# A recommender kernel on one core: gathers by a table, buffers at other addresses, a last layer in four tiles

## The chip, the cores and the metric

The kernel runs on one core of a Trainium2 chip. The metric is the device time of one execution in microseconds (us), the median of several runs. Traces come from one profiled execution. Engines: PE is TensorE (PEld its weight loads), DVE VectorE, ACT ScalarE, POOL GpSimd, SP the engine that issues most DMAs.

## What is computed

512 examples have 39 fields each. Every field looks up a row of 16 floats in its own table. Three cross layers follow, each of which multiplies every original field with every map of the layer before and mixes the products with a filter; their sums over the 16 columns, with 16 dense features, go through a small network with one output.

```python
e = stack([tbl_f[ids[:, f]] for f in range(39)], axis=1)      # (512, 39, 16)
x0 = xk = e
outs = []
for W in (f0, f1, f2):                # (39*39,128), (128*39,128), (128*39,128)
    z = einsum('bfd,bgd->bfgd', x0, xk).reshape(b, f * g, d)
    xk = einsum('bpd,pm->bmd', z, W)
    outs.append(xk)
z = sum(concatenate(outs, axis=1), axis=-1)                   # (512, 384)
h = concatenate([z, dense_ctx], axis=1)                       # (512, 400)
h = maximum(h @ W_top1 + b_top1, 0)                           # 512 wide
h = maximum(h @ W_top2 + b_top2, 0)                           # 256 wide
y = h @ W_top3                                                # (512, 1)
```

All data are float32.

## The kernel before, in words

The batch is cut into 16 chunks of 32 examples (512 columns of example and depth); the first chunk is worked on in two halves. A chunk has four subs of 8 examples, a sub has ten strips of four fields (the last has three). The 40 strips of a chunk are its slots, numbered 0 to 39, and everything else is placed at slots of this clock by hand (the tables at L158 to L190); each engine walks through the same slots in its own order, and semaphores join them.

**Layer 0** of chunk c + 1 runs during chunk c. DVE multiplies two copies of the chunk's fields (products0, L670; shifted times x0_thrice), six tiles of 117 or 128 rows, and a seventh (z_last, L681) that it splits and stacks (L692). PE multiplies each by w0 in fp32 into acc0 (L1042) and the seventh as fp32r (L1029). ACT and DVE split acc0 into x1_hi and x1_lo (L874, L712), two fp32r numbers whose sum is the value.

**Layer 1** is most of the work. For each strip PE issues three fp32r matmuls into one of seven PSUM banks (L1082, L1083, L1086): a sub's 128 columns of x1_hi or x1_lo are the stationary operand, 512 columns (384 in a last strip) of w1_hi or w1_lo the moving one. ACT (L949, four strips of each sub) and DVE (L739, six strips) scale each field's 128 columns by x0_t and add DVE's up. POOL adds the parts of ACT and DVE into x2_t (L600 twice a sub, then L607, L610 and L616).

**Layer 2** works on sums over examples and depth. At slot 9 of the next chunk PE sums a chunk's products (sum_products, L1100, 32 small matmuls on four row tiles), for which it waits for the x2_t of the last sub. After chunks 3, 7, 11 and 15 a quarter of the batch is done: at slot 13 of chunks 4, 8 and 12, and at the very end, PE runs 39 fp32 matmuls of 128 columns (layer2, L1113). During these no strip is made.

**Gathers.** POOL fetches the embedding rows with indirect DMAs (gather, L590), ten a chunk, 160 in all. The first 20 go out ahead of the loop; the rest are spread over the subs between POOL's additions. In each sub one gather follows each of the two L600, and what is left follows L616. Before the change the number comes from L641 and L642: at most AHEAD = 26 gathers ahead of the current place and at most 3 in a sub (4 in chunk 0). That makes (4, 4, 4, 4) in the four subs of chunk 0, (3, 3, 3, 1) in chunks 1 to 12 and (3, 1, 0, 0) in chunk 13.

**SP's queue.** For each chunk SP waits for its ten gathers, writes the rows to DRAM (write, L493), waits for that, and loads them in the layouts that layer 0 needs (read, L504 to L539): x0_thrice, x0_once, shifted_last, and then the shifted tiles, each when its buffer has come free. The products of chunk c start at slot 9 (11 after a quarter) of chunk c - 1, z_last at slot 6 (8).

**The top layers** run at the end, fp32r in hi and lo parts (L1165 to L1167, L1191, L1192, L1196). Their operands use the space of w1_hi, w1_lo, x1_hi and x1_lo again (L315 to L319). The last layer (L1203) is fp32: for k = 0, 1 one matmul with one weight column and 512 moving columns into one PSUM row. Each waits for its part of h2 (ACT, L1017). ACT copies the row to SBUF (L1019) and SP stores it (L576).

**Buffers.** SBUF buffers lie in the order of the sb() calls (L254 to L307), each starting at the next multiple of 32 bytes in its partition. The first call's buffer starts at byte 16,512 = 32 x 512 + 128. Small ones between the large ones (mask, roles, ids, rows, found, x0_t, x0_diag) set where the large ones begin:

```
start in a partition, and what is left modulo 512 (before the change)
w0        17056  160     z0_stack 125856  416     first, scaled, added, product       384
w1_hi     23744  192     x1_hi    127904  416     x2_t, g_sum, out0, out1, out2       384
w1_lo     43712  192     x1_lo    132000  416     wt1, wt1_dense, h1_dense, wt2       192
w2        63680  192     shifted   99232  416     z0                                  416
```

Of the kernel before, what the change touches and what calls it, by code (L numbers as in the profile page):

```python
# [8 lines left out]
I32 = mybir.dt.int32  # L9
# [21 lines left out]
H1, H2 = 512, 256  # L31
QUARTERS = BATCH // P
PER_QUARTER = CHUNKS // QUARTERS

# [3 lines left out]
E_SLOTS = 3  # L38
AHEAD = 2 * GATHERS + 6
AHEAD_OF_X1 = 2 * GATHERS - 4  # L40
GATHERS_IN_SUB = 3
GATHERS_IN_FIRST_SUBS = 4

# [199 lines left out]
def build_program(nc, a):  # L243
    with ExitStack() as ctx:
# [6 lines left out]
        def sem(name):  # L251
            return ctx.enter_context(nc.semaphore(name))

        ident = sb("ident", [P, P])  # L254
        mask = sb("mask", [P, TILE_B])
        w0 = sb("w0", [P, T0, MAPS])
# [6 lines left out]
        w0_stack = sb("w0_stack", [ROWS, MAPS], F32R)  # L263
        roles = sb("roles_sb", [ROWS, PER_TILE])
        w1_hi = sb("w1_hi", [P, FIELDS, MAPS], F32R)
        w1_lo = sb("w1_lo", [P, FIELDS, MAPS], F32R)
        w2 = sb("w2", [P, FIELDS, MAPS])


        ids = sb("ids_sb", [P, CHUNKS + 2, GATHERS], I32)  # L270
        rows = sb("rows", [P, CHUNKS, GATHERS], I32)
        found = sb("found", [P, E_SLOTS, GATHERS, D])

# [10 lines left out]
        x1_lo = sb("x1_lo", [MAPS, 2, N], F32R)  # L284

        x0_t = sb("x0_t", [P, 2, SUBS, FIELDS])
        x0_diag = sb("x0_diag", [P, SUBS, TILE_B, FG])
        first = sb("first", [P, 2, PER_STRIP, MAPS])
# [4 lines left out]
        g_sum = sb("g_sum", [MAPS, FG, P])  # L293

        out0 = sb("out0", [MAPS, BATCH])
        out1 = sb("out1", [MAPS, BATCH])
        out2 = sb("out2", [MAPS, BATCH])
        dense = sb("dense_sb", [P, QUARTERS, D])
        dense_t = sb("dense_t", [P, BATCH])
        bias1 = sb("bias1", [P, H1 // P])  # L300
        bias2 = sb("bias2", [P, H2 // P])
        wt1 = sb("wt1", [P, 3, H1])
        wt1_dense = sb("wt1_dense", [P, H1])

        h1_dense = sb("h1_dense", [P, H1 // P, BATCH])
        wt2 = sb("wt2", [P, H1 // P, H2])
        wt3 = sb("wt3", [P, H2 // P])  # L307

# [11 lines left out]
        h2 = product[:, 0:H2 // P, :, :].rearrange("p k j m -> p k (j m)")  # L320
        y = first[0:1, 0, :, :].rearrange("p j m -> p (j m)")

# [11 lines left out]
        h2_bank = [last_banks[1], last_banks[2]]  # L334
        y_bank = last_banks[3][0:1, :]

# [135 lines left out]
        def _(sp):  # L472
# [102 lines left out]
            sp.wait_ge(y_ready, 1)  # L575
            sp.dma_start(a["out"].rearrange("b o -> o b"), y).then_inc(y_out, 16)  # L576
            sp.wait_ge(y_out, 16)

        @block.gpsimd
        def _(pool):  # L580
# [57 lines left out]
            for c in range(CHUNKS):  # L638
                for s in range(SUBS):
                    u = c * SUBS + s  # L640
                    upto = min(GATHERS * c + min(GATHERS_IN_SUB * (s + 1), GATHERS) + AHEAD, CHUNKS * GATHERS)  # L641
                    left = min(GATHERS_IN_SUB if c else GATHERS_IN_FIRST_SUBS, upto - next_one)  # L642
                    for k in range(adds_of(u) - (u == LAST_SUB)):
                        add_product(u, k)
                        if left:
                            gather(next_one)
                            next_one, left = next_one + 1, left - 1
                    if u < LAST_SUB:
                        add_scaled(u)
                    for _ in range(left):  # L650
                        gather(next_one)
                        next_one += 1
# [369 lines left out]
        def _(pe):  # L1022
# [178 lines left out]
            for k in range(H2 // P):  # L1201
                pe.wait_ge(h2_ready, k + 1)
                last = pe.matmul(y_bank, wt3[:, k:k + 1], h2[:, k, :], start=(k == 0), stop=(k == H2 // P - 1))  # L1203
            last.then_inc(y_done, 1)
# [74 lines left out]
```

## Time and profile before

| | us |
|---|---|
| median of 3 runs | 645.91 (645.91 to 646.13) |
| the profiled execution, its own time | 642.16 |
| its span, first to last instruction | 640.5 |
| PE busy in it | 613.9 (96%) |
| chain that ended last | PE 59%, POOL 31%, issue 4% |

The span leaves out what lies around the program's instructions. Ends of matmuls are modelled and overlap the next one, so PE's pace is read from the distance between starts. In a merged row (x4) the first start is given. Idle time stands in brackets with the one that ended it.

### The profile page before, as it was taken

To read this page: it belongs to the slowest core of one execution; us is meant where nothing else is said; L and a number is where in the kernel's file an instruction comes from. 1 tells how busy PE (TensorE), PEld (TensorE's weight loads), DVE (VectorE), ACT (ScalarE), POOL (GpSimd) and SP (SyncE) were. 2 spreads that over 40 slices of the span, in tenths; PEclk is the share of its full clock that TensorE was granted. 3 is DMA by queue.
4 is the path that set the end of the run, shared out by engine and by line. 5 is a ranking of instruction groups with operands and counts; after the bars stand their busy time and mean duration, and the time that the engine had idled before them with its cause. 6 is when DMAs were issued, how large, how long until landed. Compare 5 with 4: busy or idle time off the path is not lost.

```text
span 640.5 us, 11151 instructions
## 1 busy us (share of the span) xinstructions
PE 613.9 (96%) x3104; PEld 469.5 (73%) x3104; DVE 546.6 (85%) x1669; ACT 360.9 (56%) x1205; POOL 511.5 (80%) x482
## 2 busy tenths in 40 slices
PE   0899899999999999999999999999999999999998
PEld 0476677677787777777788777777788777778875
DVE  4399889999986899999995899999995898988953
ACT  4255546656554565656563665656573565656733
POOL 6579899999995999999995999999995997757600
PEclk9999999999999999999999999999999999999999
DMA  7451517450511505041420505132330503100000
GB/s 237 108 151 24 141 31 224 174 152 10 129 34 11 151 6 153 7 123 40 96 66 10 152 3 141 22 97 67 67 95 3 150 12 105 54 1 2 1 2 0
DMA packets 63101, 48.86 MB, mean 76 GB/s; under 512 B 38916, under 2 KB 44428, under 8 KB 62912
## 3 DMA queue, kind: packets, MB, share of 16 engines
q1 hardware_dynamic: 56392, 42.89, 23.6%
q0 software_dynamic: 5120, 1.32, 2.7%
q10 hardware_dynamic: 1528, 3.95, 1.8%
q8 instruction: 24, 0.39, 0.3%
q14 instruction: 37, 0.30, 0.2%
HBM read 46.20 MB, written 1.94 MB: 75 GB/s over the span
## 4 chain that ended last, share of the span: by engine, by line
PE 59%; POOL 31%; issue 4%; DMA 2%; DVE 2%; ACT 1%; SPq 1%; POOLq 0%; ACTq 0%; DVEq 0%
PE strip L1082 14%; PE strip L1086 13%; PE strip L1083 13%; POOL found L590 10%; POOL added L600 9%; PE acc L1042 9%; POOL added L607 6%; PE acc L1113 4%; POOL added L610 4%; POOL x_t L616 2%; PE strip L1100 2%; PE strip L1113 1%; DVE scaled L739 1%; DMA found<-in_tables,rows 1%; ACT product L949 1%
## 5 line engine op out<-in xcount | busy, mean ns | idle before, releaser
L739 DVE SCALAR_TENSOR_TENSOR scaled<-strip,x_t,scaled 128x128 f32<-128x128 f32 x1216 | 330.8, 339 | 27.2 <-PE strip L1086 26.9
L1082 PE MATMUL strip<-w_hi,x_hi 128*128 128x512 f32 (+1 forms) x640 | 291.1, 455 | 0.7 <-ACT x_hi L874 0.7
L1086 PE MATMUL strip<-w_hi,x_lo 128*128 128x512 f32 (+1 forms) x640 | 249.4, 390 | 0.0
L1083 PE MATMUL strip<-w_lo,x_hi 128*128 128x512 f32 (+1 forms) x640 | 249.1, 389 | 0.0
L949 ACT ACTIVATE product<-strip,x_t 128x128 f32<-128x128 f32 x512 | 147.0, 373 | 113.9 <-PE strip L1086 107.5
L600 POOL TENSOR_TENSOR added<-added,product 128x512 f32<-128x512 f32 x127 | 170.0, 1339 | 49.8 <-ACT product L949 47.9
L590 POOL DMA_INDIRECT found<-in_tables,rows x160 | 167.6, 1047 | 32.5 <-issue 13.0
L1082 PEld LDWEIGHTS strip<-w_hi,x_hi 128*128 128x128 f32 x640 | 120.6, 188 | 45.6 <-issue 16.9
L1083 PEld LDWEIGHTS strip<-w_lo,x_hi 128*128 128x128 f32 x640 | 120.8, 189 | 42.7 <-issue 21.8
L1086 PEld LDWEIGHTS strip<-w_hi,x_lo 128*128 128x128 f32 x640 | 120.4, 188 | 26.1
L949 ACT ACTIVATE added<-strip,x_t 128x128 f32<-128x128 f32 x256 | 73.2, 369 | 71.1 <-PE strip L1086 71.1
L670 DVE TENSOR_TENSOR z<-shifted,x_thrice 128x512 f32<-128x512 f32 (+2 forms) x105 | 99.4, 951 | 8.1 <-DMA shifted<-x_half_fields 7.9
L1042 PE MATMUL acc<-z,w 128*128 128x512 f32 (+2 forms) x210 | 101.1, 566 | 0.6 <-DVE z L670 0.6
L739 DVE SCALAR_TENSOR_TENSOR scaled<-strip,x_t,first 128x128 f32<-128x128 f32 x256 | 71.7, 341 | 31.4 <-PE strip L1086 22.1
L607 POOL TENSOR_TENSOR added<-added,scaled 128x512 f32<-128x512 f32 x63 | 84.3, 1338 | 3.7 <-DVE scaled L739 1.0
L949 ACT ACTIVATE first<-strip,x_t 128x128 f32<-128x128 f32 x256 | 73.4, 374 | 20.5 <-PE strip L1086 11.9
L610 POOL TENSOR_TENSOR added<-added 128x256 f32<-128x256 f32 x63 | 53.4, 848 | 4.9
L1042 PEld LDWEIGHTS acc<-z,w 128*128 128x128 f32 (+1 forms) x210 | 38.6, 188 | 10.3 <-DVE z L670 3.0
L616 POOL TENSOR_TENSOR x_t<-added 128x128 f32<-128x128 f32 x63 | 35.7, 567 | 4.9
L897 ACT COPY g_sum<-strip 128x320 f32<-128x320 f32 (+2 forms) x68 | 24.5, 462 | 7.0 <-PE strip L1100 6.9
L1113 PEld LDWEIGHTS acc<-g_sum,w 128*128 128x128 f32 x234 | 26.6, 192 | 0.3
L1113 PE MATMUL acc<-g_sum,w 128*128 128x128 f32 x234 | 26.6, 275 | 0.0
(96 smaller groups left out, 253.3 us busy)
## 6 DMA issues: line engine op xcount, KB each, us to landing
shifted<-x_fields SPq DMA_DIRECT2D x91, 234.0 KB
x_thrice<-x_fields SPq DMA_DIRECT2D x29, 234.0 KB
shifted_last<-x_fields SPq DMA_DIRECT2D x14, 234.0 KB
found<-in_tables,rows POOLq DMA_INDIRECT x160, 5.6
w<-in_L_rec_f SPq DMA_DIRECT2D x1, 2496.0 KB, 11.1
g_sum<-in_L_rec_f ACTq DMA_DIRECT2D x4, 512.0 KB, 7.5
shifted<-x_fields SPq DMA_DIRECT2D x56, 22.0 KB
shifted<-x_half_fields SPq DMA_DIRECT2D x10, 117.0 KB
```

The lines of the kernel that those rows point to most:

```text
L590: pool.indirect_dma_start(out=found[:, c % E_SLOTS, k, :], out_offset=None, in_=a["tables"][:, :], in_offset=bass.IndirectOffsetOnAxis(ap= ...
L600: pool.tensor_tensor(added[:, u % 2, :, :], added[:, u % 2, :, :], product[:, product_slot(u, k) % PRODUCTS, :, :], ALU.add).then_inc(add_ ...
L607: pool.tensor_tensor(added[:, u % 2, :, :], added[:, u % 2, :, :], scaled[:, u % 2, :, :], ALU.add).then_inc(add_step, 1)
L610: pool.tensor_tensor(added[:, u % 2, 0:2, :], added[:, u % 2, 0:2, :], added[:, u % 2, 2:4, :], ALU.add).then_inc(sum_step, 1)
L670: dve.tensor_tensor(z0[of, m % Z_SLOTS, columns], shifted[of, t, columns], (x0_thrice2 if second_side else x0_thrice)[of, p, columns], ALU ...
L739: dve.scalar_tensor_tensor(into, strip[:, slot_of_strip(q) % Y_BANKS, j, :], x0_t[:, c % 2, s, f:f + 1], onto, ALU.mult, ALU.add).then_inc ...
L949: last = act.activation(into[:, j, :], strip[:, slot_of_strip(q) % Y_BANKS, j, :], ACT.Copy, scale=x0_t[:, c % 2, s, f:f + 1])
L1042: pe.matmul(acc0[:, columns_of(i)], w0[of, t, :], z0[of, m % Z_SLOTS, columns_of(i)], start=(t == 0), stop=(t == T0 - 1)).then_inc(l0_step, 1)
L1082: pe.matmul(into, x1_hi[:, c % 2, columns], hi, start=True, stop=False)
L1083: pe.matmul(into, x1_hi[:, c % 2, columns], lo, start=False, stop=False)
L1086: pe.matmul(into, x1_lo[:, c % 2, columns], hi, start=False, stop=True).then_inc(strip_ready, 1)
L1113: last = pe.matmul(acc2[quarter], w2[:, f, :], g_sum[:, f, :], start=(f == 0), stop=(f == FIELDS - 1))
```

## The change

Four edits.

1. The number of gathers in each sub comes from a table, GATHERS_IN, in place of AHEAD and the two limits. Chunk 0 has 12 instead of 16. In chunks 4, 8 and 12 the first sub has 8, 9 and 9. All other subs have at most 4. The order within a sub stays.
2. A spare buffer of 384 bytes goes in front, and the small buffers move behind the large ones. Every buffer from ident to wt2 has a size that is a multiple of 512 bytes, so each starts at a multiple of 512.
3. The last layer's matmul of 512 columns becomes four of 128, each in a column tile of its own (tile_position), with its result in PSUM row 0, 32, 64 or 96.
4. ACT copies 97 rows of 128 columns, and the store takes rows 0, 32, 64 and 96.

```diff
+Y_TILE = P // QUARTERS
+Y_ROWS = Y_TILE * (QUARTERS - 1) + 1
...
-AHEAD = 2 * GATHERS + 6
 AHEAD_OF_X1 = 2 * GATHERS - 4
-GATHERS_IN_SUB = 3
-GATHERS_IN_FIRST_SUBS = 4
+GATHERS_IN = [(4, 3, 3, 2), (3, 3, 2, 2), (3, 3, 2, 2), (3, 3, 2, 1),
+              (8, 2, 2, 2), (2, 2, 2, 2), (3, 2, 2, 2), (3, 3, 2, 2),
+              (9, 2, 2, 2), (2, 2, 2, 1), (2, 2, 2, 2), (3, 3, 2, 1),
+              (9, 2, 2, 2), (2, 2, 0, 0), (0, 0, 0, 0), (0, 0, 0, 0)]
...
+        sb("spare", [P, 3 * P // 4])
         ident = sb("ident", [P, P])
-        mask = sb("mask", [P, TILE_B])
         w0 = sb("w0", [P, T0, MAPS])
...
-        roles = sb("roles_sb", [ROWS, PER_TILE])
...
-        ids = sb("ids_sb", [P, CHUNKS + 2, GATHERS], I32)
-        rows = sb("rows", [P, CHUNKS, GATHERS], I32)
-        found = sb("found", [P, E_SLOTS, GATHERS, D])
...
-        x0_t = sb("x0_t", [P, 2, SUBS, FIELDS])
-        x0_diag = sb("x0_diag", [P, SUBS, TILE_B, FG])
...
+        dense_t = sb("dense_t", [P, BATCH])
+        wt1 = sb("wt1", [P, 3, H1])
+        wt1_dense = sb("wt1_dense", [P, H1])
+        h1_dense = sb("h1_dense", [P, H1 // P, BATCH])
+        wt2 = sb("wt2", [P, H1 // P, H2])
+        mask = sb("mask", [P, TILE_B])
+        roles = sb("roles_sb", [ROWS, PER_TILE])
+        ids = sb("ids_sb", [P, CHUNKS + 2, GATHERS], I32)
+        rows = sb("rows", [P, CHUNKS, GATHERS], I32)
+        found = sb("found", [P, E_SLOTS, GATHERS, D])
+        x0_t = sb("x0_t", [P, 2, SUBS, FIELDS])
+        x0_diag = sb("x0_diag", [P, SUBS, TILE_B, FG])
         dense = sb("dense_sb", [P, QUARTERS, D])
...
-        y = first[0:1, 0, :, :].rearrange("p j m -> p (j m)")
+        y = first[0:Y_ROWS, 0, 0, :]
...
-        y_bank = last_banks[3][0:1, :]
+        y_bank = last_banks[3][0:Y_ROWS, 0:P]
...
-            sp.dma_start(a["out"].rearrange("b o -> o b"), y).then_inc(y_out, 16)
+            sp.dma_start(a["out"].rearrange("(t b) o -> t (b o)", t=QUARTERS), y[0:Y_ROWS:Y_TILE, :]).then_inc(y_out, 16)
...
-                    upto = min(GATHERS * c + min(GATHERS_IN_SUB * (s + 1), GATHERS) + AHEAD, CHUNKS * GATHERS)
-                    left = min(GATHERS_IN_SUB if c else GATHERS_IN_FIRST_SUBS, upto - next_one)
+                    left = GATHERS_IN[c][s]
...
-                last = pe.matmul(y_bank, wt3[:, k:k + 1], h2[:, k, :], start=(k == 0), stop=(k == H2 // P - 1))
+                for t in range(QUARTERS):
+                    last = pe.matmul(y_bank[Y_TILE * t:Y_TILE * t + 1, :], wt3[:, k:k + 1], h2[:, k, P * t:P * t + P],
+                                     start=(k == 0), stop=(k == H2 // P - 1), tile_position=(0, Y_TILE * t))
```

## Rows read from the trace of the kernel before

**Rows 1.** The page's busy times, the three fullest engines: us, share, instructions.

```profile
PE 613.9 (96%) x3104; PEld 469.5 (73%) x3104; DVE 546.6 (85%) x1669; ACT 360.9 (56%) x1205; POOL 511.5 (80%) x482
```

**Rows 2.** Stretches from one summing to the next: length, busy times, clock, DMA.

```profile
core 0: us, PE busy (x) PEld busy (x) DVE busy (x) ACT busy (x) POOL busy (x), PEclk, DMA share, GB/s
...
148.54:183.21 34.67, 34.60 (x169) 26.05 (x169) 33.11 (x103) 20.96 (x72) 32.16 (x31) 1.00 0.30 76
183.21:226.50 43.29, 43.29 (x255) 35.11 (x259) 33.88 (x103) 22.13 (x76) 33.32 (x31) 1.00 0.23 61
...
553.87:587.76 33.89, 33.89 (x166) 25.73 (x166) 30.94 (x103) 21.07 (x72) 22.25 (x21) 1.00 0.00 1
```

**Rows 3.** Timeline of PE in layer 1: start, length, what; no idle time between them.

```profile
101.06 0.40 PE L1083 MATMUL strip<-w_lo,x_hi 128*128 128x512 f32 x1
...
105.03 0.34 PE L1082 MATMUL strip<-w_hi,x_hi 128*128 128x384 f32 x1
...
105.55 0.39 PE L1082 MATMUL strip<-w_hi,x_hi 128*128 128x512 f32 x1
...
127.53 1.02 PE L1042 MATMUL acc<-z,w 128*128 128x512 f32 x2
...
128.62 0.39 PE L1083 MATMUL strip<-w_lo,x_hi 128*128 128x512 f32 x1
```

**Rows 4.** Timeline of PE in the top layers.

```profile
627.21 0.39 PE L1165 MATMUL acc<-w_hi 128*128 128x512 f32 x1
...
631.74 0.40 PE L1191 MATMUL strip<-x_hi,w_hi 128*128 128x512 f32 x1
...
633.61 1.09 PE L1196 MATMUL strip<-w_lo,w_hi 128*128 128x512 f32 x4
...
634.54 1.09 PE L1196 MATMUL strip<-x_lo,w_hi 128*128 128x512 f32 x4
```

**Rows 5.** PE's waits for the last sub: total, times, longest; two summings.

```profile
PE strip L1100 <- POOL x_t L616: 4.0, 4, 2.0
...
76.53 0.35 PE L1100 MATMUL strip<-x_diag,x_t 32*128 32x80 f32 x4 [2.01 <-POOL x_t L616]
...
226.22 0.35 PE L1100 MATMUL strip<-x_diag,x_t 32*128 32x80 f32 x4
```

**Rows 6.** Timeline of POOL during layer 2 of chunk 4.

```profile
199.29 1.29 POOL L600 TENSOR_TENSOR added<-added,product 128x512 f32<-128x512 f32 x1 [6.72 <-ACT product L949]
```

**Rows 7.** Timeline at the end, a copy of 128 x 128, one summing merged.

```profile
183.21 1.13 PE strip L1100 x32
...
624.63 0.27 ACT L906 COPY out<-strip 128x128 f32<-128x128 f32 x1 [7.20 <-PE strip L1113]
...
635.50 1.27 ACT L1017 ACTIVATE product<-strip,bias 128x512 f32<-128x512 f32 x2 [4.01 <-PE strip L1196]
...
636.33 1.88 PE L1203 MATMUL strip<-product,wt 128*1 128x512 f32 x4 [0.70 <-ACT product L1017]
...
638.24 0.58 ACT L1019 COPY first<-strip 1x512 f32<-1x512 f32 x1 [1.48 <-PE strip L1203]
```

**Rows 8.** From a chunk's last gather to its use: chunk 2, then chunk 7.

```profile
69.72 0.83 SPq L525 DMA_DIRECT2D shifted_last<-x_fields  x1
...
73.28 2.08 DVE L681 TENSOR_TENSOR z_last<-shifted_last,x_thrice 117x512 f32<-117x512 f32 x1 [0.74 <-DMA shifted_last<-x_fields]
...
236.30 0.96 POOL L590 DMA_INDIRECT found<-in_tables,rows  x1 [0.15 <-POOL added L600]
...
243.77 0.83 SPq L525 DMA_DIRECT2D shifted_last<-x_fields  x1
...
248.52 0.96 POOL L590 DMA_INDIRECT found<-in_tables,rows  x1 [0.16 <-issue]
...
259.26 0.68 DVE L681 TENSOR_TENSOR z_last<-shifted_last,x_thrice 117x512 f32<-117x512 f32 x1
```

More of the change, by code:

```diff
@@ L297, in build_program @@
         out2 = sb("out2", [MAPS, BATCH])
-        dense = sb("dense_sb", [P, QUARTERS, D])
         dense_t = sb("dense_t", [P, BATCH])
-        bias1 = sb("bias1", [P, H1 // P])
-        bias2 = sb("bias2", [P, H2 // P])
         wt1 = sb("wt1", [P, 3, H1])
@@ L306, in build_program @@
         wt2 = sb("wt2", [P, H1 // P, H2])
+        mask = sb("mask", [P, TILE_B])
[5 more added lines that the diff above has]
+        x0_diag = sb("x0_diag", [P, SUBS, TILE_B, FG])
+        dense = sb("dense_sb", [P, QUARTERS, D])
+        bias1 = sb("bias1", [P, H1 // P])
+        bias2 = sb("bias2", [P, H2 // P])
         wt3 = sb("wt3", [P, H2 // P])
```

## The prediction

> **What bounds the kernel now.** The busy table comes first: PE is busy for 96% of the span, DVE for 85%, POOL for 80% [rows 1]. The reader should see that a share over the whole span can't say who leads, because DVE and POOL rest in the chunks with layer 2. So the second view is the table of stretches, cut at the summing matmuls [rows 2]. A chunk without layer 2 takes 34.67 us. In it PE is busy 34.60, DVE 33.11, POOL 32.16. A chunk with layer 2 takes 43.29 and PE is busy throughout, DVE for 33.88. A late chunk, which has no gathers left, takes 33.89, with POOL at 22.25 and DVE at 30.94. PE's granted clock is 1.00 in all three, its 2.4 GHz level. So PE leads everywhere, and DVE stands 1.5 us a chunk behind it, POOL 2.5 us.
>
> The third view is PE's own order in time, since the busy time of pipelined matmuls hides their pace. Layer 1's matmuls of 512 columns start 3.97 us / 17 = 233.5 ns apart, those of 384 columns 0.52 / 3 = 173 ns [rows 3]. The fp32 matmuls of layer 0 do better: 1.09 us from L1042 at 127.53 to the L1083 that follows holds four passes and one layer-1 matmul, so a pass takes (1090 - 233) / 4 = 214 ns [rows 3]. Layer 1 thus loses 233.5 - 214 = 19 ns on each of 1,920 matmuls against a rate that the same array reaches beside it.
>
> The end of the kernel shows that this loss has to do with which buffers are read. Twenty matmuls of one form, whose both operands lie in w1_hi and w1_lo, start 4.53 / 20 = 226.5 ns apart. From 631.74 the moving operand is x1_hi and nothing else changes: the next eight take 1.87 / 8 = 234 ns each [rows 4]. Buffers are laid out in the order of the sb() calls, each rounded up to 32 bytes, the first at byte 16,512. That puts w1_hi and w1_lo at 192 past a multiple of 512, x1_hi and x1_lo at 416. Against this reading stand the four L1196 at 633.61, which again read only w1_hi and w1_lo and take 0.93 / 4 = 232 ns [rows 4]. They follow directly on the x1 ones, and the twenty were preceded by about eight unsettled ones too, so I read 226.5 as a pace that sets in after some matmuls.
>
> **Addresses.** With 384 spare bytes in front and the small buffers at the end, every matmul operand of layer 1 starts at a multiple of 512. Stationary and moving operand then agree modulo 512, as in the twenty. The trace of before has no pair at 0 and 0, so the price is bounded: nothing (the pace has another cause), or 19 ns a matmul (the fp32 passes' 214). A loss is not excluded, but nothing in the rows points to one: PE's pace in layer 1 is the same in the first chunks and the last ones. I take 226.5, because that row is nearest: same dtype, same shape, operands that agree. It brings 233 - 226.5, say 6.1 ns after the chunk's starts (which are already faster), on 1,920 matmuls and some 50 of the top layers: 1,970 x 6.1 = **12.0 us**. Per chunk that is 0.73 us, so plain chunks go from 34.67 to 33.9, still above DVE's 33.1. The loads write the same bytes in the same order to other addresses: nothing, covered by the chunk or so that they run ahead. DVE, ACT and POOL buffers of the adds were at 384 modulo 512 and go to 0, and I take their durations as unchanged; if each DVE operation got 1% slower, 0.3 us a chunk would still be under cover.
>
> **Gathers.** Ten gathers cost POOL 32.16 - 22.25 = 9.9 us a chunk [rows 2], 1.0 us each. PE stands still for POOL only at the summing matmuls, which need the last sub's x2_t: 4.0 us in four waits, 2.01 of it at the first, while most of the seventeen, like that at 226.22, don't wait [rows 5]. The table takes 4 gathers out of chunk 0 (16 becomes 12), so POOL reaches the first sum 4 us earlier, and takes up to three out of chunks 5, 6, 9 and 10. It puts them into the first sub of chunks 4, 8 and 12, where POOL stands idle for 6.72 us while PE does layer 2 [rows 6]. The five or six more there cost 5 to 6 us, less than that idle stretch: nothing, and if the cover fails, POOL's next adds start late by at most 1 us, with product's three slots and seven strip banks between it and PE. I take **3.3 us** of the 4.0, because chunk 2's data come later at the same place (below). Bounds: 0 and 4.0. POOL's lead matters more once PE is faster: with ten gathers POOL has 32.2 us of work in 33.9.
>
> **Last layer.** L1203's four records take 428 ns each and ACT's copy starts 1.91 us after the first [rows 7]. By four column tiles each k has eight records of 128 columns. If the tiles run side by side, as the summing matmuls seem to (32 records in 1.13 us, on row tiles), k = 1 starts when ACT's second relu is done at 636.77 and ends 0.3 + 0.2 us later: 0.9 us gained. If they run one behind the other nothing is gained. The copy of 97 x 128 instead of 1 x 512 should take what L906's 128 x 128 takes, 0.27 instead of 0.58: 0.3 us. The store has four rows of 512 bytes instead of one of 2,048: nothing. I take 0.8 + 0.3 = **1.1 us**; ends 0.3 and 1.2.
>
> **Sum.** 12.0 + 3.3 + 1.1 = 16.4 us. The profiled execution took 642.16, its span 640.5; it lies 3.75 under the median of the three runs, 645.91, to which I apply the difference: **629.5 us**.
>
> **Rivals.**
> 1. *Full rate, and DVE leads.* At 0 modulo 512 the pace falls to the fp32 passes' 214. PE's plain chunk would be 34.67 - 120 x 0.019 = 32.4, below DVE's 33.1 [rows 2]. Ten plain chunks with gathers then save 1.3 each, chunks 14 and 15 2.1 each, three chunks with layer 2 2.3 each, the first chunk and the top 3: 27; with waits and last layer 4 more, less some 3 for two engines in step that are both nearly full: 28, so 618. For it: the loss of 19 ns has no other visible reason, since the granted clock is 1.00. Against: no fp32r pair in the trace reaches it. The Trainium skill (TensorE: Matmul & The Clock Gate, Back-to-back issue gap) gives N / 2.4 + 2.5 ns for an isolated stream, 216 ns at 512 columns; by that rule this rival holds if addresses are all that stands in the way, and the trace's 226.5 and 233.5 are both above it.
> 2. *Addresses do nothing.* The L1196 row is the true one and the pace depends on what ran before. Then only 3.3 + 1.1 is left: 641.5. The Trainium skill (SBUF — State Buffer, Door 1: The DMA port swizzle) speaks of 16-byte lines in SBUF; every buffer of before starts at a multiple of 32, so by that rule the move changes no line and this rival holds. The step from 226.5 to 234 at 631.74 speaks against it.
> 3. *Slower: late gathers.* A chunk's last gather moves from the second sub to the third of the chunk two ahead. For chunk 7 it was at 236.30, the load of shifted_last went out at 243.77, and DVE used it at 259.26 [rows 8]. In its new place, like the gather at 248.52, it is 12.2 later at worst, less some 2 for the gathers gone from before it: the load goes out at 254. In chunk 2, where DVE did wait for this load, issue to use took 73.28 - 69.72 = 3.6, so it is ready at 257.5, with 1.8 us to spare. If the loads take 2.6 us longer, since it shares the queue with the writes and the loads of x0_thrice ahead of it, DVE stops for 0.8 us in each of 13 chunks, and it has no slack to make it good. That is 10.4 us on top of rival 2: 652. It decides once the slack of 1.8 us is gone; in chunk 2 there is none, and the last gather there is some 2.7 us later, for which I gave 0.7 back above.
> 4. *Nothing to be told:* addresses neutral, and chunk 2's delay eats the gain at the sums: 645.
>
> **How the numbers follow.** The forecast has 0.36, rival 1 0.28, rival 2 0.24, rival 3 0.07, rival 4 0.05. A measurement of this kernel can tell about 0.2%, 1.3 us. The first three are faster; of rival 2's share 0.02 goes to the middle, since its gain could be 0.3 to 5.2, and 0.01 to slower. So faster 0.88 - 0.03 = 0.85, same 0.05 + 0.02 = 0.07, slower 0.07 + 0.01 = 0.08. The range runs from rival 1's 618 less 2 for its unknown coupling to rival 2's 641.5 plus 0.5: 616 to 642. It leaves out rivals 3 and 4 and the worst of rival 2. The forecast's own range is 626 to 633.
>
> **What would show it.** In the changed profile: L1082, L1083 and L1086 227 ns apart, plain chunks of about 33.9 us and PE the busiest; 214 to 216 ns with DVE waiting for nothing and PE for DVE would be rival 1; 233 still, rival 2. The wait for x2_t at the first sum should be gone, POOL's 6.7 us idle stretches filled with gathers, z_last waiting for its load only in chunk 2. From the first L1203 to ACT's copy 1.0 us instead of 1.9. I am wrong if PE's pace is above 233, or z_last waits in most chunks.

## The result: slower by a quarter of a per cent

The changed kernel takes 647.7 us (median of 20 runs, 643.11 to 651.4), the kernel before, beside it, 645.64 (20 runs, 644.97 to 647.34). The ratio is 1.0027, with an interval of 1.0014 to 1.0039: slower, by little, but the interval lies above 1. The forecast was 629.5, so the sign is wrong. The profiled execution took 648.34, its span is 645.2. Here and below a ratio and its interval come from the single runs and differ by up to 0.1% from the quotient of the two medians; a gain or loss in us is worked out from the ratio. One of the twelve runs of experiment 3 took 884.35 us at a granted clock of 0.66; the median given there includes it, the ratio doesn't.

The changed kernel scatters more, by 8.3 us over its 20 runs against 2.4. Its mean granted clock is 0.995; it was 0.997 in the six runs of experiment 5, which has no table, and in the eleven of the kernel before beside those.

Terms: a closing chunk is one of 4, 8 and 12, during which layer 2 of a quarter runs, the others are plain; a sum is a summing of layer 2, at slot 9. The turning of x_0, at slot 6, is four matmuls with the unit matrix that transpose x_once, a chunk's fields, for ACT and DVE to scale by.

The busy times and PE's waits of the changed kernel, the first answering to [rows 1], the wait for x_t to [rows 5], and last a wait of the kernel before (columns of a wait: us in total, times, the longest):

```profile
PE 610.5 (95%) x3116; PEld 469.0 (73%) x3116; DVE 543.3 (84%) x1669; ACT 360.9 (56%) x1205; POOL 510.1 (79%) x482
...
PE acc L1057 <- DMA x_once<-x_fields: 6.5, 5, 3.7
...
PE strip L1106 <- POOL x_t L623: 0.5, 3, 0.2
...
PE acc L1051 <- DMA x_once<-x_fields: 0.4, 1, 0.4
```

PE is busy for 3.4 us less and the span is 4.7 longer. The wait for POOL at the sums is nearly gone, as forecast. In its place stands a wait that the prediction never mentions: L1057, the turning of x_0 in PE, waits for the DMA that brings x_once, 6.5 us in five stops. In the kernel before (L1051) it was 0.4 us, in one stop.

**Pace.** Two bits of layer 1, which answer to [rows 3], then the top layers, which answer to [rows 4]; at the end the same place of layer 1 in the kernel before:

```profile
102.80 0.39 PE L1089 MATMUL strip<-w_lo,x_hi 128*128 128x512 f32 x1
...
104.64 0.40 PE L1035 MATMUL acc<-z_stack,w_stack 117*128 117x512 f32 x1
...
562.22 0.39 PE L1092 MATMUL strip<-w_hi,x_lo 128*128 128x512 f32 x1
...
563.61 0.39 PE L1092 MATMUL strip<-w_hi,x_lo 128*128 128x512 f32 x1
...
564.97 0.39 PE L1092 MATMUL strip<-w_hi,x_lo 128*128 128x512 f32 x1
...
637.22 0.39 PE L1197 MATMUL strip<-x_hi,w_hi 128*128 128x512 f32 x1
...
639.03 1.07 PE L1202 MATMUL strip<-w_lo,w_hi 128*128 128x512 f32 x4
...
639.93 1.07 PE L1202 MATMUL strip<-x_lo,w_hi 128*128 128x512 f32 x4
...
556.02 0.40 PE L1086 MATMUL strip<-w_hi,x_lo 128*128 128x512 f32 x1
...
558.82 0.40 PE L1086 MATMUL strip<-w_hi,x_lo 128*128 128x512 f32 x1
```

The eight matmuls with x1_hi moving now start 1.81 / 8 = 226 ns apart (234 before), and the four L1202 behind them 0.90 / 4 = 225 (232 before). So the move does what it was said to do. In layer 1 it does half of it: eight matmuls take 1.84 us, 230 ns each. Over the whole trace, taking every two neighbouring layer-1 records of 512 columns less than 300 ns apart, the mean falls from 232.8 (1,430 pairs) to 229.6 ns (1,420 pairs), with single distances from 224 to 242.

The new pace is not one pace. Between 562.22 and 563.61 six matmuls take 232 ns each, the next six 1.36 / 6 = 227; in the kernel before twelve in the same place take 2.80 / 12 = 233. Counted from the last interruption, which is a matmul of another layer or a strip of 384 columns, the first nine distances average 230.5 ns (1,065 of them) and the later ones 226.7 (355). In the kernel before it is 232.6 and 233.3.

**Stretches** from one sum to the next, which answer to [rows 2], with the first two and the closing chunk 8 added:

```profile
core 0: us, PE busy (x) PEld busy (x) DVE busy (x) ACT busy (x) POOL busy (x), PEclk, DMA share, GB/s
0.00:81.98 81.98, 56.99 (x213) 39.91 (x213) 56.14 (x151) 33.91 (x96) 57.33 (x60) 0.96 0.45 122
81.98:116.83 34.85, 34.46 (x171) 26.30 (x170) 30.54 (x99) 21.86 (x75) 30.65 (x29) 0.99 0.25 63
...
152.30:187.59 35.29, 34.48 (x171) 25.99 (x170) 32.90 (x107) 21.39 (x73) 30.88 (x30) 1.00 0.28 76
187.59:230.43 42.84, 42.84 (x249) 34.84 (x248) 31.41 (x101) 21.84 (x75) 35.16 (x35) 1.00 0.33 93
...
334.35:377.56 43.21, 43.09 (x248) 34.77 (x248) 32.44 (x99) 21.70 (x76) 36.43 (x36) 1.00 0.36 94
...
559.94:593.59 33.65, 33.65 (x167) 25.68 (x166) 31.77 (x103) 21.10 (x72) 21.80 (x21) 1.00 0.00 1
```

The first sum comes at 81.98 instead of 76.53. Of these 5.5 us 2.3 lie ahead of layer 1, whose first matmul starts at 30.93 instead of 28.68. The table isn't seen in that: in the profiles of experiments 1 to 8 it starts between 29.6 and 31.9, with the old table and with new ones, in those of 9 to 13 between 27.9 and 29.1. The gather-free chunk 14 is 0.24 us shorter than before (33.65 against 33.89): that is what the addresses give a chunk in which PE waits for nothing. The plain chunk that took 34.67 takes 35.29, since PE stands still in it for 0.8 us.

**The stops** at the turning of x_0, and what followed on the first; two stretches of lower granted clock, of the changed kernel and of the kernel before; the last gather of chunk 2 and its load of x_once, before (L590, L504) and after (L597, L511); then the chain behind chunk 7's last gather, which answers to [rows 8]:

```profile
77.10 1.12 PE L1057 MATMUL acc<-ident,x_once 128*128 128x128 f32 x4 [3.69 <-DMA x_once<-x_fields]
77.86 0.78 PE L1088 MATMUL strip<-w_hi,x_hi 128*128 128x512 f32 x1
...
78.86 0.63 PE L1092 MATMUL strip<-w_hi,x_lo 128*128 128x512 f32 x1
...
81.42 0.63 PE L1092 MATMUL strip<-w_hi,x_lo 128*128 128x512 f32 x1
...
149.64 0.55 PE L1057 MATMUL acc<-ident,x_once 128*128 128x128 f32 x3 [0.92 <-DMA x_once<-x_fields]
```

```profile
75.70:82.50 6.80, 5.40 (x23) 4.08 (x25) 3.51 (x10) 0.64 (x3) 2.11 (x2) 0.50 0.69 217
...
77.40:80.80 3.40, 3.40 (x20) 2.87 (x14) 1.50 (x5) 1.86 (x6) 2.92 (x4) 0.51 0.60 187
```

```profile
62.52 0.96 POOL L590 DMA_INDIRECT found<-in_tables,rows  x1 [0.16 <-issue]
...
69.34 0.33 SPq L504 DMA_DIRECT2D x_once<-x_fields  x1
...
67.16 0.96 POOL L597 DMA_INDIRECT found<-in_tables,rows  x1
...
74.73 0.33 SPq L511 DMA_DIRECT2D x_once<-x_fields  x1
```

```profile
249.52 0.96 POOL L597 DMA_INDIRECT found<-in_tables,rows  x1
...
251.85 2.50 SPq L500 DMA_DIRECT2D x_fields<-found  x3
...
257.35 0.33 SPq L511 DMA_DIRECT2D x_once<-x_fields  x1
257.72 0.82 SPq L532 DMA_DIRECT2D shifted_last<-x_fields  x1
...
263.49 0.97 DVE L687 TENSOR_TENSOR z_last<-shifted_last,x_thrice 117x512 f32<-117x512 f32 x1
```

PE stops for 3.69 us before 77.10. The granted clock is 0.50, its 1.2 GHz level, from 75.7 to 82.5, for all of the matmuls up to the sum: from 78.86 to 81.42 they start 427 ns apart, and the nine of layer 1 from 77.86 to 81.98 take 4.1 us where 2.1 would do. In the kernel before it was 0.5 too, for 3.4 us, behind PE's stop of 2.0 at the first sum. Chunk 2's last gather starts 4.6 us later than before, 2.3 of them because layer 1 began later. Smaller stops of 0.4 to 0.9 us stand in four later chunks. For chunk 7 the last gather comes at 249.52, 13.2 us later than before, some 4 of them because all comes later since the first sum, and the load of shifted_last goes out at 257.72 instead of 243.77. DVE does not wait for it even so.

**The end**, which answers to [rows 7]:

```profile
641.71 0.89 PE L1210 MATMUL strip<-product,wt 128*1 128x128 f32 x16 [0.70 <-ACT product L1023]
642.66 0.27 ACT L1025 COPY first<-strip 97x128 f32<-97x128 f32 x1 [0.52 <-PE strip L1210]
642.95 0.61 SPq L583 DMA_DIRECT2D out_y<-first  x1
```

From the first last-layer matmul to the copy 0.95 us instead of 1.91, and the copy takes 0.27 instead of 0.58, both as forecast. But from that matmul to the end of the span it is 645.2 - 641.71 = 3.5 us against 640.5 - 636.33 = 4.2, so only 0.7 of the 1.27 came through: the store gave back 0.6.

### The profile page after: what moved, and what is told of

Same layout as the page of the kernel before. It is cut to its first block, busy times and chain, and to the rows that moved or that the text cites. A ratio compares the mean times of both kernels' runs of the same rounds, so it can differ in the third digit from the quotient of the medians.

```text
span 645.2 us, 11175 instructions
## 1 busy us (share of the span) xinstructions
PE 610.5 (95%) x3116; PEld 469.0 (73%) x3116; DVE 543.3 (84%) x1669; ACT 360.9 (56%) x1205; POOL 510.1 (79%) x482
## 4 chain that ended last, share of the span: by engine, by line
PE 67%; POOL 16%; DMA 5%; issue 5%; DVE 4%; SPq 2%; ACT 1%; ACTq 0%; POOLq 0%; DVEq 0%
PE strip L1088 16%; PE strip L1092 15%; PE strip L1089 15%; PE acc L1048 10%; POOL found L597 6%; POOL added L607 4%; PE acc L1119 4%; DVE scaled L745 3%; POOL added L614 3%; PE strip L1106 2%; POOL added L617 2%; DMA found<-in_tables,rows 1%; DMA g_sum<-in_L_rec_f 1%; PE strip L1119 1%; POOL x_t L623 1%
## 5 line engine op out<-in xcount | busy, mean ns | idle before, releaser
L597 POOL DMA_INDIRECT found<-in_tables,rows x160 | 168.0, 1050 | 36.5 <-issue 15.9
L617 POOL TENSOR_TENSOR added<-added 128x256 f32<-128x256 f32 x63 | 51.4, 816 | 4.9
```

The lines of the kernel that those rows point to most:

```text
L597: pool.indirect_dma_start(out=found[:, c % E_SLOTS, k, :], out_offset=None, in_=a["tables"][:, :], in_offset=bass.IndirectOffsetOnAxis(ap= ...
L617: pool.tensor_tensor(added[:, u % 2, 0:2, :], added[:, u % 2, 0:2, :], added[:, u % 2, 2:4, :], ALU.add).then_inc(sum_step, 1)
```

## The experiments

The theory after the first look (A): the table's late last gathers make PE wait, the addresses help a little. Its rival (B): the addresses do harm. The kernels ran in four groups (experiments 1 to 4, 5 to 8, 9 to 11, 12 and 13), each on another chip and with the kernel before beside them. That took 646.47, 645.64, 641.90 and 641.66 us in the four, so only ratios are compared across groups.

**1. The addresses alone.** The order of the sb() calls and the spare bytes of the change; gathers and last layer of before.

> The kernel before with the buffers in the new order and the spare bytes, nothing else. Theory A (the new gather table makes each chunk's x0_once and shifted_last late, and PE waits for them at the turn of x0; the addresses help a little): layer-1 matmuls 229 to 230 ns apart instead of 232.8, about 6 us saved in matmuls at most, of which a part is lost to DVE, which is nearly as full as PE: 640 to 643 us, against 645.6 before. Theory B (the addresses themselves slow DVE, the loads or the waits between engines): 647 to 649.

644.03 us, ratio 0.9957 (0.9942 to 0.9972): faster by 2.8 us. B falls, and A's 640 to 643 is missed by one. But it is a quarter of the 12.0 forecast. PE now waits for POOL at the sums 5.9 us in eight stops, against 4.0 in four [rows 5]: part of what PE gains is handed to a wait.

**2. The gathers alone.**

```
-            left = min(GATHERS_IN_SUB if c else GATHERS_IN_FIRST_SUBS, upto - next_one)
+            left = GATHERS_IN[c][s]
```

> The kernel before with the new gather table alone. Theory A: 650 to 655 us, with waits of PE for x_once at the turn of x0 in the chunks whose last gather moved to the third sub. Theory B: 641 to 645, the waits at the sums gone and nothing lost.

650.42 us, ratio 1.0051 (1.0032 to 1.007): slower by 3.3 us, with the old addresses, as A had it; B's 641 to 645 falls. Its waits:

```profile
PE acc L1051 <- DMA x_once<-x_fields: 5.5, 6, 3.1
```

The wait for x_once comes with the table: neither the addresses alone nor experiment 5 has one above 0.4 us from chunk 2 on.

**3. The last layer alone.** Four tiles with tile_position, the copy of 97 rows and the store of four rows.

> The kernel before with the last layer in four column tiles and its store of four rows alone. Both theories: 0.7 us less than before (the trace after shows 3.5 us from the first matmul of the last layer to the end instead of 4.2, because the store takes 0.6 us longer than the one of a single row): 644.9. No difference would mean that the store eats all of it.

646.08 us, ratio 0.9987 (0.9975 to 0.9998): faster by 0.8 us, in agreement with the 0.7 of the trace, though the interval runs from 0.1 to 1.6 us.

**4. A table that keeps the lead.** The changed kernel, 8 and 9 gathers with the closing chunks' first subs kept, but no chunk's last gather later than before.

```
+GATHERS_IN = [(4, 4, 4, 4), (3, 3, 3, 1), (3, 3, 3, 1), (3, 3, 3, 1),
+              (8, 2, 2, 2), (2, 2, 2, 2), (2, 2, 2, 2), (2, 2, 3, 1),
+              (9, 3, 2, 2), (2, 2, 2, 2), (2, 2, 2, 2), (2, 2, 2, 2),
+              (9, 2, 2, 2), (1, 0, 0, 0), (0, 0, 0, 0), (0, 0, 0, 0)]
```

> The changed kernel with another table: 8 and 9 gathers still go into the first subs of chunks 4, 8 and 12, but no chunk's last gather comes later than the end of the second sub of the chunk two ahead, as in the kernel before (16 gathers in chunk 0 again, 10 in chunks 1 to 3, then 14, 8, 8, 8, 16, 8, 8, 8, 15, 1). Theory A: the waits for x_once go, 638 to 642 us, faster than both kernels. Theory B: as the changed kernel, 646 to 649.

644.58 us, ratio 0.9972 (0.9959 to 0.9984). No wait for x_once is left, and the sign turns, as A had it; but A's 638 to 642 is missed. Two closing chunks became longer, one of them:

```profile
330.84:374.98 44.14, 42.84 (x249) 34.84 (x248) 32.63 (x105) 22.91 (x79) 37.26 (x37) 1.00 0.26 62
```

That chunk holds 16 gathers, against 15 in the change, and PE waits for POOL at its sum, 1.29 us. Whether many gathers in a first sub do that by themselves is asked in experiment 12.

**5. Addresses and last layer, no table.** The schedule of before, written as a table: (4, 4, 4, 4), twelve times (3, 3, 3, 1), (3, 1, 0, 0).

> The changed kernel with the schedule of gathers of the kernel before (16 gathers with chunk 0, then 3, 3, 3, 1 a chunk), so addresses and last layer without the table. Theory A (the change's loss is its late gathers, addresses and last layer are gains that add): ratio 0.9957 x 0.9987 = 0.9944, about 642 us, no wait for x_once at the turning of x_0, waits for POOL's last adds at the sums of some 0.7 us in plain chunks as with the addresses alone. Theory B (the parts disturb one another, so that gains don't add): 0.997 or more, 644 us.

643.18 us, ratio 0.9959 (0.9944 to 0.9975). The interval holds both expectations, 0.9944 and 0.997, so this doesn't settle whether the gains add in full. It does give the price of the table as it stands in the change: 1.0027 against 0.9959, 0.68% or 4.4 us, give or take 1.3. Its waits for POOL and two stretches, a plain chunk and the gather-free one:

```profile
PE strip L1103 <- POOL x_t L620: 6.8, 9, 2.1
```

```profile
core 0: us, PE busy (x) PEld busy (x) DVE busy (x) ACT busy (x) POOL busy (x), PEclk, DMA share, GB/s
262.52:297.43 34.91, 34.23 (x169) 26.08 (x170) 33.59 (x106) 21.79 (x76) 32.41 (x31) 1.00 0.28 75
556.13:589.79 33.66, 33.66 (x167) 25.68 (x166) 31.78 (x103) 21.06 (x72) 21.84 (x21) 1.00 0.00 1
```

The plain chunk with ten gathers is 0.43 longer than the same chunk before, 34.48, though its matmuls are faster: PE waits 0.68 at its end for POOL's last adds. POOL's busy 32.41 of 34.91 looks like room, but at the sum it comes last.

**6. A milder table.** 6 gathers with the closing chunks' first subs, 2 with those of the plain chunks behind, last gathers kept where they were.

```
+GATHERS_IN = [(4, 4, 4, 4), (3, 3, 3, 1), (3, 3, 3, 1), (3, 3, 3, 1),
+              (6, 3, 3, 1), (2, 3, 3, 1), (2, 3, 3, 1), (2, 3, 3, 1),
...
+              (6, 3, 3, 1), (1, 0, 0, 0), (0, 0, 0, 0), (0, 0, 0, 0)]
```

> The changed kernel with a table whose running total of gathers reaches each chunk's 40 in the fourth sub, as in the kernel before: (3, 3, 3, 1) as before, but 6 with the first sub of chunks 4, 8 and 12 and 2 with the first subs of the plain chunks that follow. Theory A (a gather may move as long as the last one of a chunk doesn't come later, and what is left to win are POOL's waits at the sums): no wait for x_once, waits for POOL at the sums of plain chunks gone or below 0.2 us, closing chunks at 42.8 as with the addresses alone since 6 gathers are below what lengthened them at 8 and 9; ratio 0.993, 641.5 us, below both kernels. Rival (a first sub with more gathers delays the adds of layer 2's chunk and costs 1 us each, as in the table that keeps the lead): closing chunks at 43.5 or more and 643 to 645 us.

640.9 us, ratio 0.9926 (0.9912 to 0.994): faster than both kernels. Closing chunks took 42.75, plain ones with nine gathers mostly 34.2. A's number holds. What is left of the waits sits mainly in the first two sums (1.9 and 1.6 us) and in one of 1.1 at 411.22.

**7. x_0 turned later.** `TURN_X0_AT = (10, 11)` instead of (6, 8), the change's table kept.

> The changed kernel, its table too, but x_0 is turned with sums slots 10 and 11 instead of 6 and 8, so that the load x_once has some 5 us more. Theory A (PE's new stops are the wait for x_once at the turning, caused by the table): the waits of 3.7 us at 77.1 and of 0.4 to 1.1 at three or four later chunks go or shrink below 0.3 us each, and the first sum comes 2 to 3 us earlier; what DVE waits for shifted_last at z_last in chunk 2 stays; ratio to the kernel before 0.997 to 1.000, 644 to 645.5. Rival (the whole chain of chunk 2's loads is late, so that PE or DVE waits as long at the next point that needs them): 1.002 to 1.004, as the change.

650.11 us, ratio 1.0076 (1.0056 to 1.0097): slower still. A's forecast of the time fell, and the rival's too. What happened at chunk 2 is in two rows and a stretch:

```profile
77.14 1.13 PE L1106 MATMUL strip<-x_diag,x_t 32*128 32x80 f32 x32 [0.16 <-POOL x_t L623]
```

```profile
79.61 1.65 DVE L687 TENSOR_TENSOR z_last<-shifted_last,x_thrice 117x512 f32<-117x512 f32 x1 [3.43 <-DMA shifted_last<-x_fields]
```

```profile
77.14:117.69 40.55, 35.72 (x169) 27.39 (x169) 34.20 (x108) 22.37 (x78) 31.53 (x31) 0.96 0.29 82
```

The stop at the turning is gone and the first sum comes 4.8 us earlier, at 77.14. Then DVE waits 3.43 for shifted_last, PE behind it 4.1 for `scaled`, and the next stretch is 5.7 us longer than the change's 34.85. So the slot isn't the fault: the whole chain of chunk 2's loads is late, and whichever engine needs it first stops. That is the rival of this experiment, though its 1.002 to 1.004 is exceeded. At the second sum both kernels are equally far, 117.69 and 116.83, since layer 1 began 0.9 us later here. The rest of the loss lies in closing chunks, which took 44.3 to 45.7. There PE waits for ACT in layer 0 and layer 2; it is a side effect of the two late turnings that I didn't follow further.

**8. Every operand at 192.** Experiment 5 with 192 spare bytes more.

```
-        sb("spare", [P, 3 * P // 4])
+        sb("spare", [P, 3 * P // 4 + 48])
```

> Addresses and last layer with the schedule of gathers of the kernel before, and 192 spare bytes more in front, so that every operand of layer 1 starts at 192 past a multiple of 512 instead of at a multiple. If what counts is that both operands agree modulo 512, the pace of layer 1 stays at 229.6 ns and the top layers at 226.5, for x_1 too, and the one time is about 642. If the multiple of 512 itself counts, the pace goes back to 232 to 233 ns and the time to 645 to 646.

```profile
633.46 0.39 PE L1194 MATMUL strip<-x_hi,w_hi 128*128 128x512 f32 x1
...
635.27 1.07 PE L1199 MATMUL strip<-w_lo,w_hi 128*128 128x512 f32 x4
```

1.81 / 8 = 226 ns with x1_hi moving, the mean of layer 1 is 229.6, the one time 643.34. A multiple of 512 isn't needed. It is a single run.

**9. x_1 32 bytes past.** Experiment 5 with `sb("gap", [P, 8])` ahead of x1_hi.

> Addresses and last layer with the schedule of gathers of the kernel before, and a gap of 32 bytes ahead of x1_hi, so that x1_hi and x1_lo, and what lies behind them, start at 32 past a multiple of 512, while w1_hi and w1_lo stay at a multiple. If what counts is that stationary and moving operand agree modulo 512, layer 1's pace goes back from 229.6 to 232 to 233 ns, as in the kernel before, where they were 224 apart, and the top layers' fp32r matmuls that read x1_hi go back to 234; chunk 14 takes 33.9 instead of 33.66. If the pace stays at 229.6, something else of the new layout brought it (the buffers of DVE, ACT and POOL, or a gap of 32 being near enough).

```profile
631.25 0.40 PE L1195 MATMUL strip<-x_hi,w_hi 128*128 128x512 f32 x1
...
633.12 1.09 PE L1200 MATMUL strip<-w_lo,w_hi 128*128 128x512 f32 x4
```

```profile
553.39:587.30 33.91, 33.91 (x166) 25.77 (x166) 30.94 (x103) 21.02 (x72) 22.20 (x21) 1.00 0.00 1
```

1.87 / 8 = 234 ns, as before the change, layer 1's mean is 232.9, and chunk 14 is back at 33.91. The one time is 640.93. It is a single run again. x_1 and what lies behind it are 32 bytes further on, all else is the new layout. The buffers of DVE, ACT and POOL lie behind it too, but within one kernel, here and before, the pace changes from 226.5 to 234 just where the first matmul reads x1_hi [rows 4]. So it is x_1's place that counts.

Which rule that follows isn't settled. Four layouts were measured, w_1 / x_1 modulo 512: 0 / 0 and 192 / 192 fast, 192 / 416 and 0 / 32 slow. That fits operands that agree modulo 512, the rule that I had expected. It fits as well that both must start at a multiple of 64 bytes, as 0 and 192 do and 416 and 32 don't, or that they agree modulo 64. x_1 at 64 past with w_1 at 0 would tell them apart; it wasn't run.

**10. The kernel before once more.** No edit.

> The kernel before once more, for its profile: the one shown lies 3.5 us under the median of its runs. If that is the start, the first sum comes 2 to 4 us after 76.53 and the stretches between sums agree with the profile shown within 0.2 us each; if it is the pace or the waits in the loop, they are longer here, and comparisons of stretches between profiles are worth less.

Neither. 641.54 us, first sum at 76.70. The stretch behind it took 37.42 against 36.90, the next 34.44 against 35.11; the later ones agree within 0.2 us but for one, 34.59 against 35.02. The median of before in this group is 641.90. So the profile shown of before isn't an odd start: it looks like this group's, and it is the groups, or their chips, that differ, by 0.7%. A sum made against that profile and moved to the other median, as mine was, carries that difference unexplained.

**11. Half a sub later.** 12 gathers with chunk 0 as in the change, 6 with closing first subs, most chunks' last gathers at the start of the third sub: half a sub later than before, by one gather earlier than in the change. Chunk 2's comes where it came before.

```
+GATHERS_IN = [(4, 4, 2, 2), (3, 4, 2, 2), (3, 3, 2, 2), (3, 3, 2, 2),
+              (6, 2, 2, 2), (2, 2, 2, 2), (3, 3, 2, 2), (3, 3, 2, 1),
+              (6, 3, 2, 2), (2, 2, 2, 2), (3, 3, 2, 2), (3, 3, 2, 1),
+              (6, 3, 2, 2), (3, 2, 0, 0), (0, 0, 0, 0), (0, 0, 0, 0)]
```

> The changed kernel with a table of its own: 12 gathers with chunk 0 as in the change, 6 with the first subs of the closing chunks, and every chunk's last gather at the start of the third sub, half a sub later than in the kernel before and half a sub to a sub earlier than in the change. Theory A (from the write to the first use the loads need 11 to 12 us and the kernel before gave them 22 to 24, so some 5 us less is free; what is left to win are POOL's waits at the first three sums, 2.0, 1.8 and 0.9 us in the milder table): no wait for x_once above 0.3, the three waits below 0.5 each, ratio 0.988 to 0.990, 638.5 us, the fastest of all. Rival (chunk 2's last gather or the loads behind it still come late, or the product of half a sub's delay is a wait as before): x_once or shifted_last waited for by over 0.5 us in two or more chunks, ratio 0.993 to 1.000.

```profile
PE strip L1106 <- POOL x_t L623: 2.6, 6, 0.7
PE acc L1057 <- DMA x_once<-x_fields: 1.0, 2, 0.6
```

636.27 us, ratio 0.9916 (0.9903 to 0.993), 5.6 us below the kernel before. Both waits are small now, though x_once was still waited for by 0.6 once and PE waited at two sums for 0.6 and 0.7, so A's 0.988 to 0.990 was too much. It stands beside the milder table's 0.9926, and their intervals overlap. Some of the 5.6 is the clock: its mean over the runs is 0.9996 here and 0.9984 for the kernel before beside it, by my estimate 0.8 us of 640. The profile shows no stretch of lower clock between layer 1's start and the end, nor do those of experiments 12 and 13.

**12. Eight with the first sub.** Experiment 11 with 8 for 6, the two taken from the last two subs of the same chunk.

> The kernel of half a sub later, and nothing changed but that the first subs of chunks 4, 8 and 12 get 8 gathers instead of 6, taken from the last two subs of the same chunk; no chunk's last gather comes later. Theory A (the 8 or 9 gathers are harmless in themselves: they lie in POOL's idle stretch, and the change loses by its late last gathers): ratio 0.991 to 0.993 as with 6, closing chunks at 42.8 to 43.0. Rival (8 gathers one after the other hold up POOL's adds and with them DVE's products and layer 2's inputs, as in the table that keeps the lead, whose chunks 8 and 12 took 44.1): closing chunks 8 and 12 at 43.5 to 44.2, ratio 0.994 to 0.997.

```profile
325.10:367.84 42.74, 42.74 (x248) 34.84 (x247) 32.43 (x103) 21.95 (x75) 34.62 (x34) 1.00 0.32 87
```

636.01 us, ratio 0.9915 (0.9902 to 0.9929); closing chunks 42.74 to 42.75, PE busy throughout. Eight gathers in layer 2's shadow cost nothing, so the loss by the table isn't there. Nine weren't tried in this table. Why the closing chunks of experiment 4 took 44.1 stays open; they hold 16 and 15 gathers, these 12 or 13, and I didn't vary that number alone.

**13. Half a sub later, x_1 32 bytes past.** Experiment 11 with the gap of experiment 9.

> The kernel of half a sub later with 32 bytes ahead of x1_hi, so that stationary and moving operand of layer 1 disagree again and its pace is 233 ns. It tells what the addresses are worth once the table is sound. Theory A (PE leads where POOL has 10 gathers or fewer, so most of 1,970 x 3.3 ns = 6.4 us comes through): slower than the kernel of half a sub later by 4 to 5 us, ratio to the kernel before 0.998 to 0.999. Rival (POOL and DVE set the pace of the plain chunks, PE's gain turns into waits at the sums): slower by 2 us or less, ratio 0.994 to 0.995, and POOL's waits at the sums vanish.

639.54 us, ratio 0.9967 (0.9954 to 0.9979). Against experiment 11 that is 0.51%, 3.3 us, between the two expectations. So x_1's place is worth 3.3 us in the best table, about half of the 6.3 that 1,970 matmuls times 3.2 ns would be. POOL's waits go from 2.6 to 1.6 us and explain one of the missing three. The rest was never there to have: chunk 14, without waits, is 0.24 us shorter, and sixteen such chunks make 3.8.

## Why the prediction was wrong

**What bounds the kernel**: right in the main. PE is the busiest everywhere, and no DVE lead showed up (rival 1 falls: no two fp32r matmuls of 512 columns in the changed kernel's layer 1 start less than 224 ns apart). But "POOL 2.5 us behind" was read from busy time. What counts is when POOL's last add of a chunk ends, and there ten-gather chunks had almost nothing to spare: experiments 1 and 5 handed PE's gain to waits at the sums.

**Addresses**: the direction was right, the size was not, and this is the larger part of the miss. The step that failed is "I take 226.5, because that row is nearest", 6.1 ns on each of 1,970 matmuls. Layer 1's mean went from 232.8 to 229.6, 3.2 ns, which would make 6.3 us, not 12.0. The prediction held the reason in its hands: it read 226.5 as a pace that sets in after some matmuls, and then charged it to all of them. Three quarters of layer 1's distances are among the first nine after an interruption, where they average 230.5; only the rest run at 226.7. A chunk in which PE waits for nothing gains 0.24 us instead of 0.73, and 2.8 us came through alone. Rival 2, that addresses do nothing, is refuted by experiments 1, 8 and 9: moving x_1 by 32 bytes is enough. But "stationary and moving operand agree modulo 512" is only one of the rules that fit (experiment 9). The L1196 row that spoke against me [rows 4] goes to 225 ns when the eight matmuls ahead of it agree (the change, experiment 8) and is 233 again when they don't (experiment 9): the pace of one pair shows in the next ones, and so the row says nothing on its own address.

**Gathers**: this step decided the sign. Its first half came out: the waits at the sums are 0.5 us in all against 4.0. The 12 gathers in chunk 0 do that at the first sum, and not the stop ahead of it: experiments 7 and 11 have no such stop and wait 0.2 us or less there. The first subs' 8 hide in POOL's idle stretch (experiment 12). The second half failed. I followed the last gather of a chunk to shifted_last and DVE's z_last [rows 8], found 1.8 us to spare, and gave late gathers a chance of 0.07. Three things were wrong with that. The load of x_once goes out just ahead of shifted_last on the same queue, and its consumer is not DVE but PE, earlier: the turning at slot 6. I had named z_last alone. Chunk 2 had no slack at all, as I wrote, and I charged its 2.7 us with 0.7, although every microsecond of it stops PE, and the granted clock was low for 6.8 us around that stop. And the price per chunk that I did work out was for the wrong consumer: z_last waited in chunk 2 alone, 3.9 us, while x_once stopped PE for 0.4 to 0.9 us in four of them.

The traces give the missing slack. From the start of a chunk's last gather to the turning of its x_0 the kernel before has 20.4 to 22.9 us, but in chunk 2 9.3, and there PE waits already. In the change it is 9.3 to 9.9 for chunks 2 to 5, 8, 9, 12 and 13, and the five stops are at five of these eight. In experiment 11 these chunks but 2 have 10.9 to 11.2, and stops of 0.4 at chunk 2 and 0.6 at chunk 3 are left; in experiment 4 no chunk but 2 has less than 18.9. So gather, write and load take over 9 us here, and the change left them no more than that in eight chunks. Neither of the signs that I had named for being wrong appeared: they looked at PE's pace and at z_last.

Rival 3's mechanism (late gathers, a load that has run out of slack) is the one that decided, at another engine and at 4.4 us with the new addresses, 3.3 with the old, instead of 10.4. Not all of the 4.4 is waits that a trace shows: the profiles of the change and of experiment 5 have 10.0 and 8.6 us of PE standing still between layer 1's start and 600 us, x_once having taken the place of POOL. The lower mean clock, 0.9946 against 0.9973 over their runs, makes 1.7 us of 640 by my estimate.

**Last layer**: right up to the store. 0.96 and 0.31 us were won before it, 1.1 forecast in all; "nothing" for the store failed, it cost 0.6 (0.61 in the queue instead of 0.24, and a later end), so 0.7 to 0.8 remains.

**The sum**: measured alone, the parts are -2.8 (addresses), +3.3 (table), -0.8 (last layer), which adds up to nothing; together they are +1.7, with an interval of 0.9 to 2.5. The single parts are uncertain by about 1 us each, so this barely shows that they disturb one another. Against the forecast: addresses and last layer bring 2.6 (experiment 5) instead of 13.1, the table costs 4.4 instead of bringing 3.3. That is 10.5 and 7.7, the whole of the distance.

## What to carry to other kernels

When a prefetch moves, list every load that is queued behind it and the first consumer of each, on every engine, and take the slack of the tightest, in the chunk with the least of it; the consumer that comes to mind first is often not the first in time. Where an engine meets another at a point (here the sum), its lead is the distance between their last two instructions before it, not the difference of their busy times, and a faster leader turns into a wait once that distance is used up. A pace that was read in a long unbroken run is a bound for a stream that is broken every few matmuls, not its price. The parts of such a change are worth measuring one by one: the best kernels here keep all three, with other numbers in the table.

## What the runs showed of the hardware

Where a matmul's operands lie in a partition can set its pace. Matmuls of fp32r, 512 columns, each with a weight load, start 226.5 ns apart in the top layers when w_1 and x_1 lie at 0 / 0 or 192 / 192 modulo 512 bytes, and 232 to 234 when they lie at 192 / 416 or 0 / 32 [rows 4 and experiments 8, 9]. In layer 1 the means are 229.6 and 232.8 to 232.9, and the faster pace sets in by degrees, over some nine matmuls after each interruption. Other distances were not tried, nor is it shown why. fp32 matmuls did not change: two passes of layer 0 take 428 to 429 ns with w0 and z_0 at 160 and 416 modulo 512, and with both at 0. The Trainium skill (SBUF — State Buffer, Door 1: The DMA port swizzle) speaks of 16-byte lines; by that rule a move by 32 bytes would change nothing for a matmul, and here the measurement decides against reading it so. The Trainium skill (TensorE: Matmul & The Clock Gate, Back-to-back issue gap) gives 216 ns for 512 columns as the isolated gap of a matmul, and 131 ns sustained for pairs of weight load and matmul; no stretch of fp32r matmuls here averaged less than 226, and the measurement decides.

A stop of PE can cost more than its length. With the stop of 3.69 us the granted clock went to 0.50 for 6.8 us, and nine layer-1 matmuls took 2 us more than at the full clock. Other stops were followed by 3.4 us of it: one of 2.01 in the kernel before, one of 1.61 in experiment 5. It is not each time: after one of 1.86 at the first sum of experiment 8 the clock stayed at 1.00. In experiments 11 to 13, whose longest stop in the loop is 1.11 us, it never fell there.
